# Ten gathered tiles instead of six, counts over nine tenths of layer one, and a preparation in batches of five tiles

## The reference

```
h  = relu(layernorm(x))
x1 = x + b0 + sum over edges e into a node of W0[type(e)] @ h[src(e)]       # layer one, 8 edge types
h  = relu(layernorm(x1));  d = 1/sqrt(deg + 1)       # deg counts edges; the layer adds one more self loop
out = x1 + leaky_relu(d[dst] * (sum over edges and the self loop of d[src] * h[src]) @ W1 + b1, 0.2)  # layer two
```

## Time and profile before

| | us |
|---|---|
| median of 3 runs (lowest, highest) | 3072.77 (3071.65, 3078.24) |
| the profiled execution, its span | 3060.57, 3056.2 |
| preparation, to the first instruction of the layers | 0 to 123 |
| layer one, first sum to the last product of its last tiles | 134.6 to 2686 |
| wait for the last tile of table1, first gather of the tail | 2698.9 |
| tail | 2698.9 to 3056.2 |
| busy: PE, DVE, ACT, POOL | 2516.7, 1738.2, 1303.7, 1870.5 |

### The profile page before, as it was taken

How to read it: one execution, slowest core, us unless ns; L and a number is a source line. 1 busy time by engine, 2 the same in 40 slices (tenths; PEclk the granted TensorE clock), 3 DMA queues, 4 the chain that set the end, 5 groups by cost and what they waited for, 6 DMA issues and landing times.

```text
span 3056.2 us, 62731 instructions
## 1 busy us (share of the span) xinstructions
PE 2516.7 (82%) x21373; PEld 1731.4 (57%) x21373; DVE 1738.2 (57%) x5514; ACT 1303.7 (43%) x3284; POOL 1870.5 (61%) x1938
## 2 busy tenths in 40 slices
PE   1277777877888888898888888898899889978979
PEld 1155655655666666665666566666655555644545
DVE  6566666766666666766677666676522222221534
ACT  4444545554545454545454545454534343300000
POOL 6766666666666666665666566666666666446552
PEclk9589888989899899999999999999999999989989
DMA  6355556556656666766657665666666666557776
GB/s 214 117 153 177 169 171 210 169 177 181 206 178 198 199 194 195 223 204 195 191 178 247 186 194 181 207 193 188 202 193 194 211 192 206 156 166 227 241 245 191
DMA packets 317211, 589.69 MB, mean 193 GB/s; under 512 B 39553, under 2 KB 218512, under 8 KB 316896
## 3 DMA queue, kind: packets, MB, share of 16 engines
q0 software_dynamic: 116160, 356.96, 40.1%
q1 hardware_dynamic: 179158, 147.73, 15.4%
q10 hardware_dynamic: 21578, 80.99, 7.3%
HBM read 480.80 MB, written 104.72 MB: 192 GB/s over the span
## 4 chain that ended last, share of the span: by engine, by line
PE 63%; issue 11%; another core or an unknown queue 8%; DVE 7%; ACT 5%; DVEq 2%; DMA 1%; ACTq 0%; SPq 0%; POOL 0%; POOLq 0%
PE ps_slot L1302 14%; PE ps_slot L1335 12%; PE ps_slot L1352 11%; PE ps_proj L1321 11%; PE ps_aux L1352 11%; DVE hot_m_f L1197 3%; DVE hot_lo_f L1199 2%; ACT gap_f L1066 1%; ACT staging_f L1037 1%; PE ps_slot L1377 1%; PE ps_slot L1336 1%; PE ps_slot L1306 1%; PE ps_proj L1318 1%; ACT onehot_f L1074 1%
## 5 line engine op out<-in xcount | busy, mean ns | idle before, releaser
L923 POOL DMA_INDIRECT rows_f<-table,idxT x1815 | 1783.3, 983 | 1105.6 <-remote 420.2
L1197 DVE TENSOR_SCALAR hot_m_f<-iota_m_f,mkey 128x400 bf16<-128x400 f16 x2816 | 760.7, 330 | 294.6 <-remote 138.3
L1302 PE MATMUL ps_slot<-onehot_f,rows_f 128*128 128x128 bf16 x9702 | 702.8, 226 | 151.0 <-issue 148.7
L1335 PE MATMUL ps_slot<-hot_m_f,hot_lo_f 128*128 128x400 bf16 x2816 | 617.2, 352 | 174.3 <-ACT staging_f L1037 77.9
L1037 ACT ACTIVATE staging_f<-ps_slot 128x400 bf16<-128x400 f32 x704 | 339.7, 501 | 978.7 <-PE ps_slot L1336 468.1
L1302 PEld LDWEIGHTS ps_slot<-onehot_f,rows_f 128*128 128x128 bf16 x9702 | 602.6, 101 | 244.6 <-issue 185.3
L1066 ACT ACTIVATE gap_f<-iota,keyT 128x128 bf16<-128x128 bf16 x1617 | 526.4, 391 | 25.8 <-ACT staging_f L1037 12.6
L1143 DVE TENSOR_TENSOR acc_f<-ps_slot,acc_f 128x272 f32 (+1 forms) x605 | 247.0, 408 | 479.7 <-remote 374.8
L1335 PEld LDWEIGHTS ps_slot<-hot_m_f,hot_lo_f 128*128 128x128 bf16 x2816 | 273.9, 117 | 333.3 <-issue 177.9
L1352 PE MATMUL ps_slot<-abuf_f,stash_f 128*128 128x512 bf16 x1650 | 397.1, 391 | 18.5 <-issue 11.0
L1321 PE MATMUL ps_proj<-w0t,acc_f 128*128 128x256 f32 x1600 | 394.8, 398 | 14.6 <-issue 13.6
(11 more groups left out here) (147 smaller groups left out, 1147.4 us busy)
## 6 DMA issues: line engine op xcount, KB each, us to landing
counts_d<-staging_f ACTq DMA_DIRECT2D x88, 800.0 KB
abuf_f<-counts_d SPq DMA_DIRECT2D x110, 640.0 KB
rows_f<-table,idxT POOLq DMA_INDIRECT x1815
stash_f<-table SPq DMA_DIRECT2D x28, 960.0 KB
table<-hs SPq DMA_DIRECT2D x50, 192.0 KB, 1.9
table<-hs_f SPq DMA_DIRECT2D x50, 192.0 KB
x_d<-x_f SPq DMA_DIRECT2D x50, 128.0 KB
acc_f<-x_d SPq DMA_DIRECT2D x50, 128.0 KB
```

The costliest lines, as they stand in the source:

```text
L923: eng.indirect_dma_start(rows[:, n % RING, c, :], None, V["table0"] if n < PL.nlot else table1, bass.IndirectOffsetOnAxis(ap=idxT[:, at * ...
L1197: eng.tensor_scalar(hot_m[:, w % NHOT, j, :], iota_m[:, :], V["mkey"][:, bass.ds(first_chunk + j, 1)], float(-BIG * window), ALU.subtract, ...
L1302: last = eng.matmul(o[:, b * w:(b + 1) * w], rows[:, k, c, p * DF + b * P:p * DF + (b + 1) * P], hot[:, c, :], start=(c == 0 and p == 0), ...
L1335: eng.matmul(o[:, 0:MW], hot_lo[:, w % NHOT, :, j], hot_m[:, w % NHOT, j, :], start=(j == 0), stop=False)
```

## The change

Three edits and what they entail.

1. `GATHERED` 6 to 10. Now td = 40, 640 windows, 10 groups, 100 units, 110 gathered lots in the tail. `Plan` runs as before on the new numbers.
2. `last_window` 4/5 to 9/10 of the 539 slots: window w is in slot 2 + w*485//640, the last in slot 486. With both, the slots 2 to 432 hold 569 windows (before 704) and 433 to 486 hold 71 (before none). Layer one then holds 138 pieces, 88 of them up to slot 432 (before 85), 17 in 433 to 485 (before 34) and 33 after (before 33). The seam holds 4 as before. Slots 547 to 608 hold 58 dense pieces, four slots of small identity pieces (581 to 584) and 41 closings; 609 and 610 close four more tiles. From slot 609 to 656 there are 48 gathered lots without any dense piece; the last five tiles are closed in slots 614, 625, 636, 647 and 658. Before, dense pieces went on to slot 613, next to the last gathered lot in 612.
3. The preparation goes in ten batches of five tiles with three batch buffers. One copy or subtraction does 1280 columns in place of five that do 256; the normalised tile is written over `xres`, which takes the place of `h32` and `r1`. Every second subtraction for lo goes to DVE, ACT copies the weights, SP loads `x`, ACT's queue loads the edges, `window_starts` is issued before the last batch's store. `below` lies in the part of `xres` that is done with, so it waits for the lo parts of the first batches.

Also `acc` is no longer cleared by one memset on DVE but by four clears on ACT, among the first one-hots.

```diff
-GATHERED = 6
+GATHERED = 10
-        last_window = self.nlot * 4 // 5
+        last_window = self.nlot * 9 // 10
@@ preparation, sync
-                for t in range(T):
-                    eng.wait_ge(S["hi"], t + 1)
-                    eng.wait_ge(S["mid"], t + 1)
-                    eng.wait_ge(S["lo"], t + 1)
-                    eng.dma_start(table0[t * P:(t + 1) * P, :], hs[:, t % NH, :]).then_inc(s_t0[t % NH], 16)
-                    if t == NH + 2:
+                for li, (a, b) in enumerate(XL):
+                    if li == 3:
                         compare_ends()
-                window_starts()
+                    eng.wait_ge(S["hi"], li + 1)
+                    eng.wait_ge(S["mid"], li + 1)
...
+                    k = (li % HB) * BT
+                    eng.dma_start(table0[a * P:b * P, :].rearrange("(t p) d -> p t d", p=P), hs[:, k:k + b - a, :]).then_inc(s_t0[li % HB], 16)
+                    if li == NX - 2:
+                        window_starts()
@@ preparation, scalar
+                def first(li):
+                    eng.wait_ge(S["nbias"], li + 1)
+                    a, b = XL[li]
+                    for t in range(a, b):
+                        last = eng.activation(xres[:, t, :], xres[:, t, :], ACT.Relu, scale=rs[:, t:t + 1], bias=nb[:, t:t + 1])
+                    last.then_inc(S["h32"], 1)
...
+                    eng.activation(split(li, 0), batch(li), ACT.Copy).then_inc(S["hi"], 1)
+                def second(li):
+                    eng.wait_ge(S["r1"], li + 1)
+                    eng.activation(split(li, 1), batch(li), ACT.Copy).then_inc(S["mid"], 1)
@@ preparation, gpsimd
+                for li in range(NX):
+                    eng.wait_ge(S["hi"], li + 1)
+                    eng.tensor_tensor(batch(li), batch(li), split(li, 0), ALU.subtract).then_inc(S["r1"], 1)
+                    if li - 1 in POOL_LOWS:
+                        low(li - 1)
@@ preparation, vector (its new end)
+                scales(9)
+                for n in range(4, 6):
+                    check_part(n)
+                low(7)
+                window_firsts()
+                low(9)
+                for n in range(6, CHECK_PARTS):
                     check_part(n)
@@ both layers
             for n in range(AHEAD):
                 build_gap(n + 1)
                 build_onehot(n)
+                clear(n * P, s_zero)
...
-            eng.memset(acc[:, :, :], 0.0).then_inc(s_zero, 1)
```

More of the change, by code:

```diff
@@ L215, in _ @@
             def _(eng):
[L217 to L224, removed]
@@ L225, in _ @@
-                eng.wait_ge(S["const"], 8)
[L228 to L257, removed]
@@ new lines, in second, with copy_weights @@
+                def second(li):
+                    eng.wait_ge(S["r1"], li + 1)
+                    eng.activation(split(li, 1), batch(li), ACT.Copy).then_inc(S["mid"], 1)
+                def copy_weights(r):
+                    eng.wait_ge(S["wtp"], r + 1)
+                    eng.activation(w0t[:, r, :, :].rearrange("p b o -> p (b o)"), ps_slot[:, (n_edge + r) % 6, 0:NB * DF], ACT.Copy).then_inc(S["wcp"], 1)
+                root(0)
+                for li in range(NX):
+                    first(li)
+                    if li + 1 < NX:
+                        root(li + 1)
+                    if li > 0:
+                        second(li - 1)
+                    if li == NX - 2:
+                        for r in range(R // 2):
+                            copy_weights(r)
@@ L261, in _ @@
+                for r in range(R // 2, R):
+                    copy_weights(r)
+                second(NX - 1)
             @block.gpsimd
             def _(eng):
+                eng.memset(xres[:, 0, :], 0.0).then_inc(S["memx"], 1)
+                eng.memset(xres[:, T - 1, :], 0.0).then_inc(S["memx"], 1)
                 eng.memset(er[0][:, full, :], int(PAD_DST)).then_inc(S["padm"], 1)
@@ L371, in copy, with low, window_firsts @@
                         eng.memset(small[:, 5, 0:1], 0.0).then_inc(S["rel"], 1)
-                    else:
-                        eng.tensor_copy(w0t[:, i - n_edge, :, :].rearrange("p b o -> p (b o)"),
-                                        ps_slot[:, i % 6, 0:NB * DF]).then_inc(S["ecp"], 1)
+                def low(li):
+                    eng.wait_ge(S["mid"], li + 1)
+                    eng.tensor_tensor(split(li, 2), batch(li), split(li, 1), ALU.subtract).then_inc(S["lov"], 1)
+                def window_firsts():
+                    eng.wait_ge(S["wst"], 1)
+                    step(eng.tensor_copy(wst[:, :], wst_i[:, :]))
+                    for q in range(BELOW_X):
+                        if q in POOL_LOWS:
+                            eng.wait_ge(S["lo"], lows_of_pool(q))
+                        else:
+                            eng.wait_ge(S["lov"], lows_of_dve(q))
+                    for i in range(KC):
+                        last = eng.tensor_scalar(below[:, i, :], wst[:, :], ends[:, 1, i:i + 1], None, ALU.is_gt)
+                    last.then_inc(S["below"], 1)
                 def check_part(n):
@@ L398, in check_part @@
                     elif n == 9:
-                        eng.wait_ge(S["wst"], 1)
-                        step(eng.tensor_copy(wst[:, :], wst_i[:, :]))
-                    elif n == 10:
-                        for i in range(KC):
-                            last = eng.tensor_scalar(below[:, i, :], wst[:, :], ends[:, 1, i:i + 1], None, ALU.is_gt)
-                        last.then_inc(S["below"], 1)
-                    elif n == 11:
-                        pass
-                    elif n == 12:
@@ new lines, in _ @@
+                stats(4)
+                scales(3)
+                edge_offsets()
+                edge_keys()
+                stats(5)
+                scales(4)
+                edge_sources()
+                low(1)
+                stats(6)
+                scales(5)
+                for i in range(2 * KT):
+                    copy(i)
+                stats(7)
+                scales(6)
+                low(3)
+                stats(8)
+                for i in range(2 * KT, n_edge):
+                    copy(i)
```

182 lines of the change are left out of this document (101 added, 81 removed).

## The result

| | before | after |
|---|---|---|
| median of five runs each, us | 3071.65 | 3225.52 |
| the profiled execution, its span | 3060.57, 3056.2 | 3227.93, 3226.2 |
| first gather of layer one | 124.45 | 124.76 |
| first gather of the tail | 2698.87 | 2706.91 |
| tail | 357.3 | 519.3 |

The ratio is 1.0486 (95% interval 1.0467 to 1.0505): slower, as forecast, but 3225 lies far outside 3035 to 3165. In the profiled execution the tail grew by 162 us (forecast 123), layer one gained nothing (forecast 81), and the preparation gained nothing (forecast 12). The spans differ by 170 us and the medians by 154, because the profiled execution of the kernel before was 11 us faster than its median and that of the kernel after 2 us slower.

A forecast was written before the change was run, and what follows sets the result against it. Layer one was taken as bound by engines waiting on each other, then by PE, and the tail's end by POOL's gathers. Terms -14 - 81 + 0 + 123 = +28 gave a median of 3101 us, range 3035 to 3165.

The forecast's parts named there:

- What bounds the kernel: Layer one: engines hold each other up around tile ends, 4.65 us a slot; PE bounds from slot 433 on.
- The tail up to the last covered slot: Tail, slots 547 to 608: lot 61 is summed 310 us after the first gather, and lot 67 may be gathered.
- 43 lots at 3.75: Tail's end, lots 67 to 109: POOL's gathers alone set the pace, 161 us, with 9 us of end behind them.
- PE ending last in the tail: Tail: the prediction called itself wrong altogether if PE, and not POOL, ends last there.
- rival 3: Tail's end: gathers slow PE down, two or three times in 160 us of gathers; +35 us, 3136; chance 0.07.
- Layer one, -81: Slots 2 to 432: 135 windows fewer at 0.60 us each save 81 us (0 to 243).
- rival 2: Layer one: slots keep 4.65 us, windows matter as little as dense pieces; sum +109 us, 3182; chance 0.12.
- seven slots in eleven: Layer one: slots with no tile to finish, where PE's list runs without holes; ground for 0.60 us a window.
- 433 to 486, 0: Layer one, slots 433 to 486: 71 windows more and 17 pieces fewer cancel out, 0 us (-10 to +15).
- Preparation, -12: Before the layers: DVE becomes the bound, busy 88 us; preparation ends at 111 instead of 123 (-20 to 0).
- The memset's removal: Start of layer one: 7.31 us ahead of PE's first lot go; gain taken as 2 us (-7 to +2).
- Sum: Whole kernel: preparation and start -14, layer one -81 and 0, tail +123, together +28 us.

The follow-up runs named there:

- experiment 3: POOL pausing after gathers: in the last 48 lots of the kernel after, 1.0448 of before; in all layer-one lots of the kernel before, 0.9913.
- third kernel of experiment 1: The kernel before with only the new preparation (six gathered tiles, counts up to slot 432): 0.9993 of the kernel before.
- experiment 5: The kernel with only the new preparation, each POOL subtraction of 1280 columns cut into five of 256: 0.9964 of the kernel before, 0.9952 when measured again.
- replaced lots: The kernel after, gathers of its last 43 lots replaced by POOL's constant fills, 1.0321 of before, or by ACT's plain loads, 1.0113; kernel after beside them 1.0473.

## Why the forecast was wrong, step by step

**What bounds the kernel.** "PE alone is not the bound; the engines hold each other up around the end of every tile" was half of it. On a chip without gaps the same layer one has a slot of 3.95 us. From lot 11 to lot 433 that is 1698 us against 1998; the counted gaps are 36 us against 182, so 146 of the 300 us are gaps. That the rest is what they delay is argued, not shown.

**The tail up to the last covered slot: right.** Lot 67 was gathered at 3024.4, 317.5 us after the first (forecast 310).

**43 lots at 3.75: the step that failed in the tail.** They took 3024.4 to 3213.6, 189 us or 4.40 a lot, +28. "At which PE only looks on" is where it went wrong: PE busy is 31% there, not under 20%, and POOL waited 33 of the 202 us for it ("remote" and L1359). The prediction named PE ending last in the tail as a sign of being wrong altogether, and by experiment 3 it came. The end took 12.6 us instead of 9. 7 + 28 + 4 = 39 us, the difference between 162 and 123. It was rival 3, with the place right: the gathers slow PE down. The stretch that the rival was read from bears it out: the three slots at the tail's start, 28.8 us in the earlier trace rows with 13 us of gaps, take 13.3 us and have no gap in the third kernel of experiment 1, the very 13 that the prediction called their worth. Its price was the error: not "two or three times", it came all the way; and it doesn't hang on gathers "without a break" (experiment 3). Without gaps the 3.75 hold.

**Layer one, -81: the larger error.** From lot 11 to lot 433 it took 1997.9 us before and 1999.7 after, with 135 windows fewer. That is rival 2: with gaps a removed window is worth about nothing, and removing three quarters of all 704 is worth 65 us, 0.09 each. The step that failed is "135 x 0.60": it took PE's own time for a window to come back as time of the kernel. The two stretches, before and after (columns of the earlier trace rows), show where it went:
```profile
194.60:2192.50 1997.90, 1690.99 (x14895) 1222.91 (x14894) 1354.88 (x4566) 1019.81 (x2581) 1263.21 (x1270) 0.94 0.63 192
191.10:2190.80 1999.70, 1651.01 (x14280) 1187.60 (x14279) 1176.33 (x3911) 964.00 (x2453) 1259.17 (x1271) 0.92 0.62 188
```
135 windows at 0.71 less three pieces at 3.24 should have taken 86 us off PE; 40 went, as the granted clock fell from 0.94 to 0.92 (an estimate from these rows: 0.940 to 0.917 of 2000 us is 46 us of full clock less, and PE, busy 0.83 of the time, loses some 38 of them). And the gaps grew by more than those 40, from 182 to 255 us. Two pairs on one chip each, experiment 5's kernel (its layer one is that of before) and the kernel after, say the same: gaps 143 to 206 and 184 to 246 us, the stretch 9 and 6 us shorter. Why fewer windows leave more gaps is open. Without gaps a window is worth about 0.4 as long as the slot is above POOL's 3.75 and some. I took 0.60 because seven slots in eleven "run without holes"; the trace had 26 us of gaps in 200:400, in pauses of "issue" to which the prediction gave no price. The Trainium skill's rule that rival 2 rested on (Perfetto Trace Analysis, section Identifying the Most-Contended Engine) pointed the right way here. It doesn't tell the two kinds of chip apart: without gaps the weight loads are busy 66% of 200:400, and a window is worth 0.4.

**433 to 486, 0: it cost 12.8** (239.0 to 251.8), at the upper end of its bounds. Layer one as a whole, first gather to first gather, took 7.7 us more: 3.8 less up to lot 11, then 1.8 and 12.8 more, and 3.0 less behind lot 486.

**Preparation, -12: failed, and the cause is shown.** DVE was the bound as forecast, but busy 101 us to 124, not 88. Two rows of the kernel after:
```profile
58.00 2.61 POOL L324 TENSOR_TENSOR xres<-xres,hs 128x1280 f32<-128x1280 f32 x1 [8.11 <-ACT hs L269]
...
58.37 2.26 DVE L391 SCALAR_TENSOR_TENSOR nb<-mv,rs 128x5 f32<-128x5 f32 x1
```
Five elements a row take 2.26 us: the instruction ends when POOL's ends. Alone it takes 0.17. The Trainium skill, SBUF — State Buffer, section Who interferes with whom, has a DVE instruction with two inputs in SBUF contend with a GpSimd instruction that reads SBUF, over a pair of ports that is locked for one of them; the trace agrees, and the price is what is left of POOL's instruction, which the change had made five times as many columns. The `nb` alone make 12.4 of the 14 us by which DVE's busy time exceeds that of the cut kernel, 87 us, in which the layers begin at 112.4: the forecast's 88 and 111. The memset's removal brought 4.2 us at the first lot (10.1 us after the first gather before, 5.95 after; forecast 2), of which 3.8 were still there at lot 11.

**Sum.** Forecast 123 - 81 - 14 = +28; measured in the profiled executions 162 + 8 = +170 of span. 81 + 8 of the 142 us between them are layer one, 39 the tail and 14 the preparation.

## What to carry to other kernels

Before a wait is called "issue" and passed over, count it: where PE started one to four matmuls every 0.7 us while POOL gathered, it was held up and not at work, and most of the work removed from it came back as pauses or as a lower granted clock. Don't leave a stretch of gathers with nothing but short matmuls beside it, and time a change on more than one chip. When POOL's work is put into longer instructions, look at the DVE instructions with two inputs beside it: `nb` went from 0.33 to 1.57 us on the average.

## What the runs showed of the hardware

- The same kernel took 2628 and 2630 us on two chips and 3030, 3032 and 3076 on three others. The difference goes with the gaps in PE's issue. What decides is open; each of these chips was seen on one occasion only, so chip and occasion are not told apart.
- In the replaced lots the gaps need POOL's gathers: 191 of them with, 4 and 6 without, though DMA traffic was 348 GB/s in the last. The Trainium skill, Runtime: NRT & Kernel Launch, section Instruction fetch mechanics, has instruction fetch stream by itself, mostly hidden. The packets of the larger instruction queue, which I take to be PE's, took about as long in both kinds of chip (mean 1.07 to 1.09 us with gaps, 1.07 without), so a slow fetch transfer isn't what the traces show. Whether the sequencer or something before it stands was not found.
- Half the clock doesn't make them: without gathers the same lots ran at 0.50 of the clock without gaps.
- With less to do, PE was granted less clock: 0.94 to 0.92 with 135 windows fewer, 0.98 to 0.89 with three quarters of every window gone (lots 11 to 433), and its busy time fell by 40 and 235 us, where its own rows say 86 and 373.
